# Taylor sums as three float16 passes on scaled high and low halves, the u and delta products one group ahead, and the weight preparation moved into the first SwiGLU group

## The reference, cut to what matters

```python
approx_up = hidden_states @ up_w.T                       # u, 128 columns
delta = hidden_states @ gate_w.T - local_point
keep = abs(delta) <= 2.5
approx_out = approx_up @ local_approx_output.T
for m in 1..6:                                           # exp(m log|delta| - discount) = |delta|^m / m!
    tmp = delta**m * exp(-discount[m-1]) * approx_up     # times keep for m > 4
    approx_out += tmp @ fuse_weight[:, :, m-1].T
ffn_out = (silu(x @ ffn_gate_w.T) * (x @ ffn_up_w.T)) @ ffn_down_w.T    # 1248 hidden columns
x = layernorm(x + approx_out + ffn_out)
inter = x @ c1_w.T @ c2_w.T ; pick the argmax of every 32 columns       # 1792 hidden columns
x = layernorm(x + relu(x @ w1.T)[picked] @ w2t[picked])
```

## Time and profile before

| | |
|---|---|
| median of three runs | 806.66 us |
| span of the profiled execution | 807.3 us |
| PE busy | 776.2 us (96%) |
| DVE busy | 490.2 us (61%) |
| ACT busy | 193.2 us (24%) |
| POOL busy | 117.4 us (15%) |
| phase 0, PE's first matmul to the first of phase 1 | 4.24 to 134.14 us |

### The profile page before, as it was taken

How to read it: one execution, slowest core, us unless ns; L and a number is a source line. 1 busy time by engine, 2 the same in 40 slices (tenths; PEclk the granted TensorE clock), 3 DMA queues, 4 the chain that set the end, 5 groups by cost and what they waited for, 6 DMA issues and landing times.

```text
span 807.3 us, 12766 instructions
## 1 busy us (share of the span) xinstructions
PE 776.2 (96%) x3680; PEld 364.1 (45%) x3680; DVE 490.2 (61%) x848; ACT 193.2 (24%) x300; POOL 117.4 (15%) x108
## 2 busy tenths in 40 slices
PE   7999999799999999999999998999999999999994
PEld 3444444344444444444444444454445444444441
DVE  3479997265587778677777788545654561116104
ACT  3010246114532221222222221221222121222220
POOL 0000000111111111111111111222122112222210
PEclk9999999899999999999999999999999999999997
DMA  8951002600000000000000000000100010001001
GB/s 303 427 211 45 1 0 91 274 1 0 0 1 1 1 0 0 0 0 0 0 1 1 0 1 0 2 1 1 52 0 0 0 53 0 0 1 53 0 0 52
DMA packets 8763, 31.78 MB, mean 39 GB/s; under 512 B 800, under 2 KB 1440, under 8 KB 8224
## 3 DMA queue, kind: packets, MB, share of 16 engines
q1 hardware_dynamic: 8736, 31.42, 10.1%
HBM read 27.22 MB, written 4.19 MB: 39 GB/s over the span
## 4 chain that ended last, share of the span: by engine, by line
PE 83%; DVE 9%; issue 4%; ACT 1%; DMA 1%; SPq 1%; DVEq 0%; POOL 0%; ACTq 0%; POOLq 0%
PE acc L328 27%; PE pa L316 20%; PE pb L316 20%; PE acc L353 9%; PE pick_b L380 1%; DVE small L869 1%; DVE rows L727 1%; PE pick_a L370 1%; PE pb L341 1%; PE pa L341 1%; DMA big<-in_fuse_t 1%; PE pick_a L388 1%; DVE rows L895 1%; PE pa L474 1%; PE pick_b L388 1%
## 5 line engine op out<-in xcount | busy, mean ns | idle before, releaser
L328 PE MATMUL acc<-big,work 128*128 128x512 f16 (+1 forms) x1128 | 254.6, 379 | 0.0
L316 PE MATMUL pa<-xs,big 128*128 128x512 f16 (+1 forms) x816 | 189.8, 383 | 9.5 <-ACT work L605 5.2
L692 POOL TENSOR_TENSOR work<-work 128x512 f32 x96 | 114.3, 1191 | 558.3 <-ACT work L610 256.5
L316 PE MATMUL pb<-xs,big 128*128 128x512 f16 (+1 forms) x816 | 187.3, 379 | 0.7 <-DVE work L852 0.7
L328 PEld LDWEIGHTS acc<-big,work 128*128 (+1 forms) x1128 | 108.7, 98 | 123.3
L316 PEld LDWEIGHTS pa<-xs,big 128*128 128x128 f16 (+1 forms) x816 | 79.3, 98 | 105.3 <-issue 15.1
L316 PEld LDWEIGHTS pb<-xs,big 128*128 128x128 f16 (+1 forms) x816 | 78.8, 98 | 91.2 <-issue 1.9
L353 PE MATMUL acc<-big 128*128 128x512 f32 x224 | 97.0, 593 | 1.5 <-DVE rows L727 1.1
L1015 DVE TENSOR_TENSOR big<-rev,winner 128x1024 bf16<-128x1024 f16 x28 | 34.1, 1219 | 76.6 <-PE pb L474 76.6
L353 PEld LDWEIGHTS acc<-big 128*128 128x128 f32 x224 | 42.3, 190 | 55.9 <-issue 53.5
L663 ACT ACTIVATE work<-pa 128x512 f32<-128x512 f32 x28 | 16.7, 597 | 174.9 <-PE pa L474 174.9
(11 more groups left out here) (85 smaller groups left out, 556.6 us busy)
## 6 DMA issues: line engine op xcount, KB each, us to landing
big<-in_w_all SPq DMA_DIRECT2D x2, 3840.0 KB, 21.4
big<-in_w_all SPq DMA_DIRECT2D x2, 3584.0 KB, 15.8
rows<-in_x SPq DMA_DIRECT2D x4, 1024.0 KB, 16.7
big<-in_x_t SPq DMA_DIRECT2D x3, 1024.0 KB, 10.4
out<-rows SPq DMA_DIRECT2D x3, 1024.0 KB, 4.3
big<-in_fuse_t SPq DMA_DIRECT2D x2, 768.0 KB, 7.6
big<-in_x_t SPq DMA_DIRECT2D x4, 256.0 KB, 3.9
out<-rows SPq DMA_DIRECT2D x4, 256.0 KB, 2.4
```

Of the source, the lines that this page charges most:

```text
L316: mm = nc.tensor.matmul(dst[:, :], weights(wp)(kc * P, P), x_part16(g, xp, kc), start=(kc == 0 and wp == xp), stop=(stop and kc == KC - 1 ...
L328: mm = nc.tensor.matmul(acc[t][:, :], act_part(pair, j, ap, t * P, P), weights(wp)(0, H), start=(first and ap == wp), stop=(last and ap == 1))
L692: nc.gpsimd.tensor_tensor(act_part(pair, j, 1), act32[j], act_part(pair, j, 0), ALU.subtract).then_inc(act_lo, 1)
```

## The change

1. **Taylor products in float16.** Every term and every fuse weight is scaled by a power of two and split into a float16 high and low half. Each float32 matmul becomes three float16 matmuls (L398 after). Of a group the scale comes from a bound on its terms: the largest |u| and |delta| of each partition (`measure`, `bound_terms`), reduced over the partitions on POOL as ("t", g) in `MAX_ORDER`. ACT copies u with the scale and casts each term (`terms_high`), POOL subtracts (`terms_low`) and also forms keep and delta x keep (`keep_delta`). Terms live in a ring of three buffers: DVE may write term n when POOL has done with term n-3. Descaling is in `take_taylor`.
2. **u and delta a group ahead.** `up_and_delta(g + 1)` stands ahead of `taylor(g)` on PE, with the banks `pick_a` and `pick_b` for odd groups.
3. **Weight preparation.** Before phase 1 only two slots of `w1` are split; the rest follows between the units of group 0 (`W1_PLAN`), as do the low halves of x for groups 2 and 3 and the last step of c2. The maximum over `w1` is taken in six pieces between terms of groups 2 and 3. The scale of `w2` moves to unit 3, its split to the units 4 and 5 (7 slots each, before 5, 5 and 4). The load of the first half of `w2` waits for x's last low half, that of the second half for the last low half of `w1`.
4. **Three slices by masks of -1 and 0**: `stack_z` has four instructions where it had seven, c2 four large ones (two of them on ACT) where it had eight on DVE.

```diff
-MAX_ORDER = [("x", 0), ("c1", 0), ("x", 1), ("w", 0), ("x", 2), ("w", 1), ("x", 3), ("w", 2)]
+MAX_ORDER = [("x", 0), ("t", 0), ("x", 1), ("c1", 0), ("t", 1), ("x", 2), ("t", 2), ("x", 3), ("t", 3), ("w", 0), ("w", 2)]
...
-        W2_UNIT, W2_FIRST = 5, 2
-        W1_EARLY = 3
+        W2_UNIT, W2_FIRST = 7, 3
+        W1_PLAN = ((0, 2), (2, 4), (4, 6), (6, 8), (8, 10))
...
+            load_w1(0)
+            for g in (2, 3):
                 sp.wait_ge(delta_pre_ready, g - 1)
                 sp.wait_ge(xlo_ready, g - 1)
                 load_xt(g)
+                load_rows(g - 1)
+            load_w1(1)
             load_rows(3)
             sp.wait_ge(taylor_ready, GROUPS * TPG)
             sp.wait_ge(xlo_ready, GROUPS)
-            sp.wait_ge(w1_lo, 3 * C1)
             for i in range(2):
+                if i:
+                    sp.wait_ge(w1_lo, 3 * C1)
...
+            def taylor(g):
+                for m in range(TERMS):
+                    pe.wait_ge(term_lo, g * TERMS + m + 1)
+                    if g == 0:
+                        pe.wait_ge(fuse_lo, m + 1)
                     for t in range(TPG):
-                        mm = nc.tensor.matmul(acc[t][:, :], term[m][:, t * P:(t + 1) * P], fuse[m],
-                                              start=(m == 0), stop=(m == G))
+                        for tp, fp in ((0, 0), (0, 1), (1, 0)):
+                            mm = nc.tensor.matmul(acc[t][:, :], term_part(m, tp, t * P, P), fuse_part(m, fp),
+                                                  start=(m == 0 and tp == fp), stop=(m == G and tp == 1))
...
+            up_and_delta(0)
             for g in range(GROUPS):
-                phase0(g, g % 2)
+                if g + 1 < GROUPS:
+                    up_and_delta(g + 1)
+                taylor(g)
...
+            for u in range(U1):
+                pe.wait_ge(w1_lo, 3 * 2 * (u + 1))
+                unit1(0, u, start=(u == 0))
+                if u == 1:
+                    pe.wait_ge(banks_added, added(0, GROUPS - 1, TPG - 1))
+                if u:
+                    down(0, u, "first" if u == 1 else "middle")
...
+            def terms_high(g):
+                act.wait_ge(u_ready, g + 1)
+                act.wait_ge(term_scaled, g + 1)
+                act.activation(term[g * TERMS % RING], u_bank(g)[:, :], ACT.Copy, scale=t_in[:, g:g + 1]).then_inc(u_copied, 1)
+                for m in range(TERMS):
...
+                    act.activation(term_part(m, 0), term[n % RING], ACT.Copy).then_inc(term_hi, 1)
+                    if g == 0 and m < G:
+                        fuse_high(m + 1)
...
+            for u in range(U1):
+                swiglu(0, u, start=(u == 0), weights=0 if u == U1 - 1 else None)
+                if u == 1:
+                    x_hi(2, 0)
+                    x_hi(3, 1)
+                if u < 3:
+                    w1_high(*W1_PLAN[2 + u])
+            swiglu(1, 0, weights=W2_UNIT)
...
+            def terms_low(g):
+                for m in range(TERMS):
+                    n = g * TERMS + m
+                    pool.wait_ge(term_hi, n + 1)
+                    nc.gpsimd.tensor_tensor(term_part(m, 1), term[n % RING], term_part(m, 0), ALU.subtract).then_inc(term_lo, 1)
+                    keep_delta(g, m)
+
-            for i in range(7):
+            for i in range(len(MAX_ORDER) - 1):
                 reduce_max(i)
+                if MAX_ORDER[i][0] == "t":
+                    terms_low(MAX_ORDER[i][1])
...
+            def make_terms(g):
+                for m in range(1, TERMS):
+                    n = g * TERMS + m
...
+                    if n >= RING:
+                        dve.wait_ge(term_lo, n + 1 - RING)
+                    if m == 5:
+                        dve.wait_ge(kept, g + 1)
+                    v.tensor_tensor(term[n % RING], term[(n - 1) % RING], delta_keep if m >= 5 else delta,
+                                    ALU.mult).then_inc(terms_ready, 1)
+                    if g == 0:
+                        fuse_low(m)
+                    else:
+                        between_terms(g, m)
...
+            for g in range(GROUPS):
+                if g == 1:
+                    x_low(0)
+                x_max(g)
...
+                measure(g)
...
+                bound_terms(g)
+                scale_terms(g)
+                power_scales(x_all[:, g:g + 1], x_exp[:, g:g + 1], x_scale[:, g:g + 1], x_inv[:, g:g + 1], x_scaled)
+                make_terms(g)
+            v.tensor_reduce(w_part[:, 0:1], w1_part_max, axis=AX.X, op=ALU.max).then_inc(max_part, 1)
+            scale_phase1()
+            scale_phase1_sums()
+            w1_low(*W1_PLAN[0])
+            take_taylor(GROUPS - 1)
...
+            for u in range(U1):
+                if u == 0:
+                    w1_low(*W1_PLAN[1])
+                swiglu(0, u, 0)
+                if u == 3:
+                    w2_max(0)
+                    w2_max(1)
+                if u == U1 - 1:
+                    w2_low(0, W2_FIRST)
+                swiglu(0, u, 1)
+                if u == 1:
+                    x_low(2)
+                    x_low(3)
+                if u < 3:
+                    w1_low(*W1_PLAN[2 + u])
+                if u == 0:
+                    stack_c2()
+                if u == 3:
+                    w2_max(2)
+                    w2_max(3)
+                    scale_phase2()
```

More of the change, by code:

```diff
@@ L53 @@
 W2_SLOT, W1_SLOT = 2 * H, 3 * H
+W2_SHIFT = 2 * W2_SLOT
 W2_AT = 0
@@ L144, in program @@
         ve, y, ya = small[:, 32:36], small[:, 36:40], small[:, 40:44]
+        t_part, t_all = small[:, 0:4], small[:, 4:8]
+        t_exp, t_scale, t_inv, t_in = small[:, 8:12], small[:, 12:16], small[:, 16:20], small[:, 20:24]
+        f_part, f_max, f_exp, f_scale, f_inv = small[:, 24:27], small[:, 27:28], small[:, 28:29], small[:, 29:30], small[:, 30:31]
+        fuse_scale = small[:, 31:31 + TERMS]
+        u_max, d_max, d_two, k_two, factor_max, silu_first = [small[:, i:i + 1] for i in range(38, 44)]
         def words(at, n):
@@ L149, in program, with fuse_part, term_part @@
         xt = [words(XT_AT + i * KC * GT, KC * GT) for i in range(2)]
-        fuse = [words(FUSE_AT + m * H, H) for m in range(G + 1)]
+        fuse_raw = [words(FUSE_AT + (m + 1) * H, H) for m in range(TERMS)]
         ug = words(UG_AT, KC * 2 * S)
-        term = [words(TERM_AT + m * GT, GT) for m in range(G + 1)]
-        delta, keep, delta_keep = [words(DELTA_AT + i * GT, GT) for i in range(3)]
+        def fuse_part(m, part):
+            at = 2 * (FUSE_AT + m * H) + part * H
+            return big16[:, at:at + H]
+        def term_part(m, part, a=0, n=GT):
+            at = 2 * (TERM_AT + m * GT) + part * GT + a
+            return big16[:, at:at + n]
+        term = [work32[:, i * GT:(i + 1) * GT] for i in range(RING)]
+        delta, keep, delta_keep = [work32[:, (RING + i) * GT:(RING + i + 1) * GT] for i in range(3)]
         w1_raw = words(W1_AT - W1_SLOT, C1 * W1_SLOT)
-        w2_raw = words(W2_AT + W2_SLOT, C2 * W2_SLOT)
+        w2_raw = words(W2_AT + W2_SHIFT, C2 * W2_SLOT)
         def w1_part(s, k, part):
@@ L555, in _, with fuse_high @@
             act.wait_ge(vectors_in, 16 * 2)
-            def copy_u(g):
-                act.wait_ge(u_ready, g + 1)
-                act.activation(term[0], pa[:, :], ACT.Copy).then_inc(u_copied, 1)
             act.activation(factor, disc_sb[:, :], ACT.Exp, scale=-1.0).then_inc(factor_ready, 1)
-            act.wait_ge(factor_ready, 1)
-            for m in range(1, G + 1):
-                act.wait_ge(fuse_in[1 + (m > 3)], 16)
-                if m == 3:
-                    copy_u(0)
-                act.activation(fuse[m], fuse[m], ACT.Copy, scale=factor[:, m - 1:m]).then_inc(fuse_scaled, 1)
+            act.activation(silu_first, disc_sb[:, 0:1], ACT.Silu)
+            def fuse_high(m):
+                if m:
+                    act.wait_ge(fuse_lo, m)
+                act.activation(fuse_part(m, 0), fuse_raw[m], ACT.Copy, scale=fuse_scale[:, m:m + 1]).then_inc(fuse_hi, 1)
             def x_hi(g, i):
@@ L685, in reduce_max @@
                 what, col = MAX_ORDER[i]
-                part, whole = {"x": (x_part, x_all), "w": (w_part, w_all), "c1": (c1_part, c1_all)}[what]
+                part, whole = {"x": (x_part, x_all), "t": (t_part, t_all), "w": (w_part, w_all), "c1": (c1_part, c1_all)}[what]
                 pool.wait_ge(max_part, i + 1)
@@ new lines, in fuse_low, with between_terms @@
+            def fuse_low(m):
+                dve.wait_ge(fuse_hi, m + 1)
+                v.scalar_tensor_tensor(out=fuse_part(m, 1), in0=fuse_raw[m], scalar=fuse_scale[:, m:m + 1], in1=fuse_part(m, 0),
+                                       op0=ALU.mult, op1=ALU.subtract).then_inc(fuse_lo, 1)
+            def between_terms(g, m):
+                if g == 1:
+                    if m == 1:
+                        take_taylor(0)
+                    elif m == 2:
+                        x_low(1)
```

(23 more changed lines are left out.)

390 lines of the change are left out of this document (218 added, 172 removed).

## The result

The changed kernel took 826.54 us (median of four runs, 825.89 to 828.0) against 807.05 us for the kernel before beside it: a ratio of 1.0229 (95% interval 1.0211 to 1.0247). It is slower by 18.5 us by that ratio (the medians lie 19.5 us apart), and the forecast was 827 us.

A forecast was written before the change was run, and what follows sets the result against it. PE bounded the kernel before; after, POOL, switching between reductions and subtractions, stands in the chain feeding PE. Phase 0 +14.8, phase 1 +6.7, `stack_z` -1 give +20.5 us on 806.7: 827 us, range 808 to 840.

The forecast's parts named there:

- S0, the first subtraction: POOL's first subtraction in group 0 of phase 0, forecast at 35.9 us (31.4 with the shorter switch).
- POOL's turn: POOL's switch between reduction and elementwise work: 3.8 to 11.9 us each; 11.9 taken for the first to subtraction.
- Periods: Phase 0, from each group's first subtraction to the next: 31.6, 28.2, 27.6 us, then 25.6 us to phase 1.
- Start of phase 1: End of phase 0: phase 1 starts at 148.9 us against 134.1, +14.8 us.
- The signs: Expected in the profile: subtractions 7 us or more late, PE idle about 12 and 9 us, phase 1 near 149 us.
- Phase 1, group 0: New waits in group 0 of phase 1 less 7 us given back: +6.7 us, bounds 0 and +12.
- The old hole: PE's 5.19 us wait for a late silu at 155 us plus 2.6 us slow clock; 7 of 7.8 us given back.
- Unit 3: Phase 1, group 0: w2's maximum on DVE delays products; PE stands about 5 us, plus 2.6 for the clock.
- The split of w2: Phase 1, group 0: 14 pairs per unit, 13.3 us of 15.5; silu(10) and silu(12) late by 1.3 us each.
- Silus behind w1's and x's splits: Phase 1, group 0, ACT: silu(0), silu(2), silu(4) queue behind high halves, costing PE about 1, 1.5 and 1 us.
- Hidden turns: Rival: POOL's switches are hidden and PE bounds phase 0; 782 to 806 us, middle 795, chance 0.14.
- Mutual slowing of DVE and POOL: Rival: DVE and POOL slow each other throughout; +25 us at most, 852, half of it 840; over 836: chance 0.13.

The follow-up runs named there:

- experiment 2: Changed kernel plus a one-column POOL subtraction ahead of each group's first in phase 0 and behind w1's reduction: 826.47 us, ratio 1.0207.
- experiment 1: Changed kernel without phase 0's reductions over partitions, each partition using its own maximum (part of the computation left out): 799.48 us, ratio 0.9884.
- experiment 3: Kernel before plus one single-column POOL subtraction behind its last reduction ahead of phase 1: 801.59 us, ratio 0.9913.
- experiment 11: Changed kernel with phase 0 subtractions on DVE, splits dealt by column, one-column POOL subtraction, group 2's banks taken behind group 3's first term: 801.69 us, ratio 0.9913.
- experiment 5: Changed kernel with phase 0's subtractions and keep product on DVE, POOL only reducing there: 806.45 us, ratio 0.9967.

## Why the prediction came true, step by step

- **Taylor products: right.** 18.1 us per block predicted, 18.29 measured at full clock.
- **S0, the first subtraction: put 7.5 us too late** (35.9 predicted, 28.37 measured). The step that failed is "POOL's turn ... I take 11.9 us (7.4 is the other end)", paid after the demand at 23.9. The turn took 8.17 us, and it began at the end of the reduction, 2.3 us ahead of the demand, since its instruction stands ahead of the wait there. The prediction even argued from the loop of the kernel before that lead does not help; experiment 2 shows that this holds only in the loop, and the list of POOL before, ahead of the prediction, has the wait in front of the instruction without operands there. The high half was 1.4 us earlier as well.
- **Periods: right in kind, put 0.4 to 2.2 us too short each.** 31.6, 28.2, 27.6 and 25.6 predicted; 32.0, 29.8, 29.0 and 27.8 measured (60.34 - 28.37 and so on). The turn back was priced at 3.8 and took 5.8 to 8.0. The 3.8 was counted from the demand at 183.28 us, but the turn had begun at the end of the subtraction before: the row itself shows 5.55 us of idle time. It is the same mistake as with S0, made the other way. POOL's subtraction was priced at 1.3 and took 1.34 in the mean (DVE's product beside it 1.06 instead of 0.69), but its tensor_scalar, for which no row existed, 1.5 to 3.2:

```profile
93.94 3.16 POOL L782 TENSOR_SCALAR work<-work 128x512 f32<-128x512 f32 x1
...
L794 POOL TENSOR_TENSOR big<-work,big 128x512 f16<-128x512 f32 x28 | 37.1, 1336 | 35.4 <-issue 22.3 <-ACT big L640 12.7
```

- **Start of phase 1: +14.8 predicted, +12.7 measured.** The 7.5 us too much and the 5.5 us too little in the four periods nearly cancelled. (The terms given for the last period add up to 26.0, not 25.6.)
- **The signs.** Holes of PE ahead of groups 0 and 3 with a slow clock behind them came, with 3.8 and 11.1 us instead of 12 and 9. First subtractions 7 us or more behind their high half did not come; it was 4.5 to 5.9 us, since the turn began with the end of the reduction. DVE's product was to be late by 5 us in unit 3 or 4, and PE waited 0.97 and 2.51 us for it.
- **Phase 1, group 0: +6.7 predicted, 4.8 measured (with the -1 for `stack_z`, +5.7 predicted).** The old hole went as forecast. Unit 3 was over-sized: some 5 + 2.6 us predicted for w2's maxima, 0.97 us measured at 219 us. The split of w2 was under-sized: 2.6 predicted, 1.19 + 1.79 + 2.51 us and 1.7 for the clock measured. Of these the 2.51 us has a second part: behind the last pairs DVE still takes the four banks and the statistics of the layer norm (249.53 to 255.15 us) ahead of the product; in the kernel before the same work cost PE 0.67 us. Silus behind w1's and x's splits: 3.5 predicted, 1.47 + 1.46 + 1.18 measured.
- **The total was met in part by luck.** That turns of POOL would make the kernel slower, and why, was right. But S0 and phase 1 were put too high by 7.5 and 0.9 us and the periods too low by 5.5, so the span was forecast 2.9 us too long (827.8 against 824.9 us). The step from span to time had an error of its own: a run's time is 1.8 us above its span (826.67 and 824.9 us), so by the same difference the profiled execution of the kernel before, with its span of 807.3, stands for a time of about 809.1 us, above all four of its timed runs. The medians therefore lie 19.5 us apart where the spans lie 17.6. That the forecast met the median within 0.5 us is chance.
- **Rivals.** Hidden turns fell: with the turns out, the time was 799.5 (experiment 1), inside that rival's 782 to 806, so its price was right and its condition not met. Its mechanism was there: in straight code the turn does run while DVE and ACT work, but they gave it only 2.3 us. Mutual slowing of DVE and POOL is there, but the periods were 0.4 to 2.2 us longer than forecast, where that rival wanted 7.5.

What the float16 passes themselves are worth can be read from experiments 1 and 3, each without the harmful turns: 799.5 against 801.6 us, with intervals that overlap, and the first leaves the reductions out. 24 us less PE work brought phase 1 from 133.5 to 123.3 us; part of the rest went into a wait of 5.9 us for a load and blocks at the slower clock. Phase 1's new holes took the 10.2 us back: group 1 starts at 240.62 us in the profile of experiment 1 and at 240.57 in that of experiment 3.

## What to carry to other kernels

When POOL changes between a reduction over the partitions and elementwise work, count the changes per iteration before anything else: a cheap operation moved there cost two changes of about 6 to 8 us each. Where such a change can't be avoided and the operation stands in a loop, call one tiny operation of the new kind behind the last of the old. That gave 7 us ahead of a loop (experiment 3) and nothing in straight code (experiment 2). When PE gets faster, list for every engine what it must do per group: the next bound is there. Moving a wait within the list of the bounding engine brought nothing (experiment 11).

## What the runs showed of the hardware

- The turn from a reduction to elementwise work took 6.7 to 8.5 us in all cases shown here but one, which took 11.9. Back to a reduction it took 5.8 to 5.9 us in four of the five of the profile after (two of these end with a wait for DVE, so 5.8 is their upper bound), and 8.0 in the fifth, under 331 GB/s of transfers. The Trainium skill (GPSIMD Engine Reference, 2.1 Instruction dispatch) gives about 6 us for the first call to a freshly loaded kernel, with no visible instruction. The rows agree that nothing is shown and that it takes at least about as long, and they show that it recurs at every change of kind. Whether it is such a load, they don't show.
- DVE and POOL slowed each other: DVE's product of 128x512 took 1.06 us beside POOL's work and 0.68 beside an idle POOL (experiment 5), POOL's subtraction 1.34 in the mean and 1.16 where DVE was idle.
- Whether the lead is used depends on where the instruction without operands stands: ahead of the semaphore wait in straight code, behind it in a loop (experiment 2).
- The granted clock fell to the level of 1.2 GHz behind holes of 3.8 and 11.1 us, where the Taylor blocks took 20.9 and 20.4 us instead of 18.3, but not behind the one of 3.5 us at 91.33. The hole of 2.51 us at 256.08 was followed by a block with a mean clock of 0.60 (4.44 us instead of 2.75), the like hole of 2.50 us in experiment 2 by one at full clock. Of the stretches behind these holes (columns: busy of the engines, clock, DMA share, GB/s):

```profile
29.60:32.60 3.00, 3.00 (x8) 1.07 (x9) 2.98 (x3) 0.63 (x1) 2.91 (x3) 0.50 0.17 72
...
91.30:96.60 5.30, 5.27 (x24) 2.21 (x24) 5.22 (x3) 0.63 (x1) 5.21 (x3) 1.00 0.01 2
122.60:127.60 5.00, 5.00 (x14) 1.84 (x15) 5.00 (x5) 0.63 (x1) 4.83 (x5) 0.57 0.01 3
```

What tells these cases apart was not tried.
